# Adding a half head's three parts on TensorE and keeping the attention output in columns

## What is computed

```python
x = x + 0.5 * ffn(layernorm(x))     # shared experts of width 704, top 2 of 8 routed experts of width 352
x = x + attention(layernorm(x))
x = x + 0.5 * ffn(layernorm(x))

# attention: sequences of s tokens, 16 query heads and 4 key heads of 32
q = (x @ Wq.T).reshape(b, s, 16, 32);  k, v = (x @ Wk.T), (x @ Wv.T)   # 4 heads each
q, k = rope(q), rope(k)
attn = softmax(q @ k.T * 32 ** -0.5)
out = (attn @ v) @ Wo.T
```

## Time and profile before

| | |
|---|---|
| median of three runs | 1663.07 us (1660.93 to 1664.69) |
| the profiled execution | 1678.58 us, span of the core 1676.7 us |
| TensorE matmul | busy 1602.0 us (96%) |
| TensorE weight load | busy 1171.4 us (70%) |
| VectorE | busy 889.7 us (53%) |
| ScalarE | busy 649.7 us (39%) |
| GpSimd | busy 920.0 us (55%) |
| mean granted TensorE clock | 0.983 |

### The profile page before, as it was taken

One profiled execution on the slowest core, in us unless ns is written; L12 is line 12 of the kernel. 1 busy time (PEld: TensorE's weight loads), 2 busy tenths in 40 slices (PEclk: granted clock), 3 DMA queues, 4 the chain that ended last, 5 costly groups with the idle time before them and its releaser, 6 DMA issues.

```text
span 1676.7 us, 24265 instructions
## 1 busy us (share of the span) xinstructions
PE 1602.0 (96%) x8548; PEld 1171.4 (70%) x8548; DVE 889.7 (53%) x1534; ACT 649.7 (39%) x974; POOL 920.0 (55%) x754
## 2 busy tenths in 40 slices
PE   6998999999998898999999999989999999999997
PEld 5776799999986774444444444337778788999985
DVE  5553322222267687888888887656554432222236
ACT  4421222323232415656666566653541222323320
POOL 3106294503766856777778778750314366533635
PEclk9999899999999999999999999999999999999998
DMA  9306454423363331010010110004103455333337
GB/s 339 123 12 231 152 187 137 175 76 129 123 210 111 82 74 41 21 38 20 23 37 20 26 33 1 20 7 154 56 1 121 144 226 179 133 130 129 135 95 238
DMA packets 67841, 175.69 MB, mean 105 GB/s; under 512 B 10769, under 2 KB 11665, under 8 KB 65425
## 3 DMA queue, kind: packets, MB, share of 16 engines
q1 hardware_dynamic: 54896, 100.48, 18.5%
q0 software_dynamic: 12832, 73.67, 12.4%
HBM read 102.29 MB, written 55.84 MB: 94 GB/s over the span
## 4 chain that ended last, share of the span: by engine, by line
PE 78%; DMA 8%; DVE 5%; ACT 3%; issue 3%; POOL 2%; SPq 1%; DVEq 0%; POOLq 0%; ACTq 0%
PE PS L1117 10%; PE PS L1119 10%; PE PS L1118 10%; PE PS L1350 8%; PE PS L1331 8%; PE PS L1364 6%; PE PS L1373 5%; DMA xn<-x_routed 4%; DMA xs<-x_routed 2%; PE PS L1254 2%; PE PS L1259 2%; PE PS L1257 2%; PE PS L1256 2%; PE PS L1255 2%; PE PS L1258 2%
## 5 line engine op out<-in xcount | busy, mean ns | idle before, releaser
L1610 ACT ACTIVATE PT<-PS 128x1024 f32<-128x1024 f32 x256 | 258.0, 1022 | 157.6 <-PE PS L1350 155.4
L1907 DVE TENSOR_REDUCE nmf_later<-PS 128x1 f32<-128x1024 f32 x160 | 192.1, 1217 | 47.7 <-PE PS L1331 47.7
L1364 PE MATMUL PS<-PT,V 128*32 128x512 f32 x1024 | 203.4, 607 | 0.0
L943 POOL TENSOR_TENSOR added<-PT 128x1024 f32<-128x1024 f32 x60 | 146.3, 2439 | 102.7 <-ACT PT L1610 102.7
L1968 POOL TENSOR_TENSOR W<-raw,W 128x544 fp32r<-128x544 f32 x144 | 190.1, 1352 | 1.5
L1350 PE MATMUL PS<-QS,KS 98*128 98x512 f32 x512 | 181.7, 438 | 1.6 <-DVE nmf_later L1907 1.3
L1331 PE MATMUL PS<-KS,QS 96*128 96x512 f32 x512 | 168.7, 411 | 4.7 <-ACT PT L1610 2.3
L1874 DVE TENSOR_TENSOR thid<-thid,PS 128x352 f32<-128x352 f32 x78 | 40.6, 521 | 247.3 <-ACT thid L1541 247.3
L1350 PEld LDWEIGHTS PS<-QS,KS 98*128 98x128 f32 x512 | 80.5, 191 | 106.2 <-issue 50.0
L1956 POOL DMA_DIRECT2D raw<-ffn_w x18 | 10.0, 555 | 257.6 <-POOLq L1954 193.6
L1117 PE MATMUL PS<-xh,W 128*128 128x512 f32 x352 | 141.4, 402 | 5.6 <-ACT hid L1532 2.1
(11 more groups left out here) (197 smaller groups left out, 3874.1 us busy)
## 6 DMA issues: line engine op xcount, KB each, us to landing
raw<-ffn_w POOLq DMA_DIRECT2D x18, 2176.0 KB, 10.3
y_routed<-ytile SPq DMA_DIRECT2D x78, 256.0 KB, 2.1
xn<-x_routed SPq DMA_DIRECT2D x40, 256.0 KB, 3.4
x_routed<-xq SPq DMA_DIRECT2D x1, 9984.0 KB, 29.3
xs<-x_routed SPq DMA_DIRECT2D x38, 256.0 KB, 3.6
QS<-later_hi SPq DMA_DIRECT2D x112, 64.0 KB, 2.0
raw<-ffn_w SPq DMA_DIRECT2D x6, 768.0 KB, 10.0
raw<-ffn_w SPq DMA_DIRECT2D x16, 272.0 KB
```

Source lines behind the costliest of these rows:

```text
L943: e.tensor_tensor(to, PT[:, (u + 1) % PTBUF, :], PT[:, (u + 2) % PTBUF, :], ALU.add).then_inc(done.sem, 1)
L1364: e.matmul(PS[i * QUARTER:(i + 1) * QUARTER, ob, :], V[:, b * QT + kt, g, :], PT[:, u % PTBUF, kt % 2 * GRP:(kt % 2 + 1) * GRP], start=rou ...
L1610: e.activation(PT[:, u % PTBUF, :], PS[:, i:i + 2, :].rearrange("p b n -> p (b n)"), ACT.Exp, scale=SCALE).then_inc(p_ready.sem, 1)
L1907: e.tensor_reduce(row_maxima(n)[:, h, t:t + 1], PS[:, i:i + 2, :].rearrange("p b n -> p (b n)"), AX.X, ALU.max, negate=True).then_inc(max_ ...
```

## The change

Nothing is transposed any more between the values and the projection. The sums' matmul takes 32 columns of ones and writes the sum to all 32 rows of quarter 3. `store_head` is one matmul of OT's first 96 rows against `thirds`, three identities of 32 one below the other, into quarter 2 of the bank MISC; it stands ahead of the last value round of the half head after. VectorE takes the reciprocal of OT's quarter 3, 32x512, in an item of its own (`invert`, after the fourth unit), and multiplies PSUM by it straight into qtok, which now holds columns (32 partitions of a head, 512 tokens). ScalarE copies 128 rows to OT and waits for the reciprocal of the half before. `turn_heads` becomes `split_heads`: ScalarE and VectorE split from SBUF, without TensorE. `place_max` moves from a half head's fourth unit to the next one's first, `turn_queries` and `place_queries` two units later.

```diff
-        if outputs and pair == 0:
-            work.append(("store_head", *outputs.pop(0)))
-        if hh >= 0 and pair in (1, 2):
-            work.append(("values", hh, pair))
+        if hh >= 0 and pair == 1:
+            work.append(("values", hh, 1))
+        if hh >= 0 and pair == 2:
+            if hh:
+                work.append(("store_head", hh - 1))
+            work.append(("values", hh, 2))
+        if hh >= 0 and pair == 3:
+            work.append(("invert", hh))
...
-            e.matmul(PS[SUMS_ROW:SUMS_ROW + 1, ob, :], one_col[:], src,
+            e.matmul(PS[SUMS:, ob, :], ones[:], src,
...
-            for j in range(TPG):
-                mm = e.transpose(PS[:, MISC, j * P:j * P + SUMS_ROW + 1], OT[0:SUMS_ROW + 1, j * P:(j + 1) * P],
-                                 identf[0:SUMS_ROW + 1, 0:SUMS_ROW + 1])
+            e.matmul(PS[SUMMED, MISC, :], thirds[:], OT[0:SUMS, :],
+                     start=True, stop=True).then_inc(parts_summed.sem, 1)
...
-            e.activation(OT[0:SUMS_ROW + 1, :], PS[0:SUMS_ROW + 1, out_bank(n, hf), :],
+                act.wait_ge(parts_summed, hh - 1)
+                act.wait_ge(inverted, hh - 1)
+            e.activation(OT[:], PS[:, out_bank(n, hf), :], ACT.Copy).then_inc(ot_ready.sem, 1)
...
-            dve.step(e.reciprocal(rL[:, q, :], o[:, :, 0, 3]))
-            e.tensor_reduce(head[:, q, :, :], o[:, :, :, 0:3], AX.X, ALU.add).then_inc(halves_summed.sem, 1)
+            dve.wait_ge(parts_summed, hh)
+            dve.wait_ge(inverted, hh)
+            e.tensor_tensor(qtok[h * HD:(h + 1) * HD, t0:t0 + TPG, g * P:(g + 1) * P],
+                            PS[SUMMED, MISC, :].rearrange("p (j n) -> p j n", n=P),
+                            rL[SUMMED, :].rearrange("p (j n) -> p j n", n=P), ALU.mult)
...
+            elif kind == "invert":
+                dve.wait_ge(ot_ready, hh)
+                    dve.wait_ge(head_ready, hh - 1)
+                e.reciprocal(rL[SUMMED, :], OT[SUMS:, :]).then_inc(inverted.sem, 1)
...
-                to_columns(3, t, qtok[:, t, :], 4 + t % 4)
+                e.activation(XH[g][:, :, cols], qtok[:, t, :].rearrange("p (c n) -> p c n", c=DC),
+                             ACT.Copy).then_inc(x_hi.sem, 1)
```

More of the change, by code:

```diff
@@ L48 @@
 QUARTER = P // 4
-SUMS_ROW = 3 * QUARTER
+SUMS = 3 * QUARTER
+SUMMED = slice(2 * QUARTER, 3 * QUARTER)
 QKV = D + 2 * NKV * HD
@@ L421, in order_of_work @@
     work.append(("heads_start",))
-    outputs, maxima, lows = [], [], []
+    maxima, lows = [], []
     groups = len(KV_GROUPS)
@@ L457, in order_of_work @@
     hh = end // (QT // 2) - 1
-    work.extend([("sum", hh), ("values", hh, 0), ("store_head", *outputs.pop(0)), ("values", hh, 1), ("values", hh, 2),
-                 ("store_head", *half_head(hh))])
+    work.extend([("sum", hh), ("values", hh, 0), ("values", hh, 1), ("store_head", hh - 1), ("values", hh, 2),
+                 ("invert", hh), ("store_head", hh)])
     work.append(("attention_end",))
@@ L470, in order_of_work @@
         if i < NT:
-            work.append(("turn_heads", turned[i]))
+            work.append(("split_heads", turned[i]))
         if i >= 2:
@@ L586, in macaron @@
     nmf_first, behind = place("nmf_first", (P, REP, QT), F32, behind)
-    one_col, _ = place("one_col", (P, 1), F32, behind)
+    ones, behind = place("ones", (P, QUARTER), F32, behind)
+    thirds, _ = place("thirds", (SUMS, QUARTER), F32, behind)
     ropeS, _ = place("ropeS", (P, QT, 2, HD), F32, at)
@@ L612, in macaron @@
     MT, at = place("MT", (QT, 2, 2, P), F32, at)
-    rL, at = place("rL", (P, 2, TPG), F32, at)
-    head, at = place("head", (P, 2, TPG, HD), F32, at)
+    rL, at = place("rL", (P, GRP), F32, at)
     nmf_later, at = place("nmf_later", (P, 2 * REP, QT), F32, at)
@@ L865, in macaron @@
                 x_back[g].plan()
[L866 to L867 removed]
+        elif kind == "split_heads":
+            for a in (x_hi, x_lo):
                 a.plan(3, *key)
@@ L962, in macaron @@
     place_place = {key: i for i, key in enumerate(placed)}
[L963 to L966, removed]
     def slots_over(lane):
@@ L974, in heads_over @@
         lane.wait_ge(pv_done, last_half, 2)
-        lane.wait_ge(ot_turned, *heads[-1])
-        lane.wait_ge(ot_ready, *ends[-1])
-        lane.wait_ge(head_ready, *heads[-1])
+        lane.wait_ge(head_ready, last_half)
         lane.wait_ge(wo_ready, DC - 1)
@@ L2024, in gpsimd_program @@
             elif kind == "value_ones":
-                e.memset(one_col[:], 1.0).then_inc(v_ones.sem, 1)
+                for i in range(3):
+                    of = slice(i * QUARTER, (i + 1) * QUARTER)
+                    pool.step(e.tensor_copy(thirds[of, :], identf[of, of]))
+                    pool.after_step()
+                e.memset(ones[:], 1.0).then_inc(v_ones.sem, 1)
                 pool.wait_ge(v_ones)
```

76 lines of the change are left out of this document (35 added, 41 removed).

## The result

The changed kernel takes **1817.83 us** (median of 4 runs, 1811.97 to 1822.26) beside 1662.97 for the kernel before on the same chip: a ratio of 1.093, 95% interval [1.089, 1.097]. It is slower by 9%. The prediction was 1815 us. The profiled execution took 1814.38 us, its span is 1812.6.

A forecast was written before the change was run, and what follows sets the result against it. The prediction took TensorE to bound the kernel before, and VectorE with its long reciprocal after. Its terms, 139 + 16 - 3 = +152 us, added to the median of 1663.07, gave 1815 us, range 1740 to 1870.

The forecast's parts named there:

- the bound moves to VectorE: Attention, per half head: VectorE needs 8.8 us of work against 7.4 for TensorE, so VectorE becomes the bound.
- the loop: Attention: scores of unit 2 wait for maximum 0 behind the reciprocal; period 9.24 us, TensorE idle about 1.67 per half head.
- The reciprocal: VectorE, 32x512 per half head: 6.75 ns per element over 146 ns, 3.6 us, from a line through two small sizes.
- the rival that takes the small rows for a fixed start: VectorE: 512 elements take about 0.7 us, TensorE stays the bound; 1640 us, chance 0.08.
- the one with 8.4 ns: VectorE: reciprocal slower per element, 4.4 us for 512, 0.8 more per half head; 1863 us, chance 0.12.
- The clock: TensorE after stalls: 1.34 us lost per drop, in two half heads of three, 0.89 per half head; period 10.13.
- The rival's price: Attention: TensorE's clock stays up in spite of the stalls; 1760 us, chance 0.17.
- the term of 139: First seven groups: period from 7.65 to 10.13 us over 56 half heads, drops of the clock included; +139 us.
- The last group: Sums' matmul waits for VectorE's additions behind the reciprocal, 2.8 us, four times: 11, with clock drops 16 us.
- The end: Last OT copy and output projection: +1.7 us for the longer path, -4.7 for the transposes gone; -3 us.
- The matmul with `thirds`: TensorE: 0.01 us beside its neighbours; the rival has it run alone, 0.98 us, 1870 us in all, chance 0.07.
- The faster case: Attention: a cheap reciprocal, below about 2 us, leaves TensorE the bound; 1640 us, chance 0.08.

The follow-up runs named there:

- busy2: Changed kernel with the maximum matmuls of each half head's second unit issued three times in place of once; 1768.53 us, ratio 1.065 to the kernel before.
- r384: Changed kernel, reciprocal covering only 384 of 512 columns from the second half head on (2.55 us); 1721.96 us, ratio 1.036 to the kernel before.
- r4: Changed kernel, reciprocal covering only 4 of 512 columns from the second half head on (0.17 us); 1644.54 us, ratio 0.989 to the kernel before.
- split4: Changed kernel with the reciprocal cut into four of 128 columns, one behind each of the half head's four maxima; 1853.59 us, ratio 1.108 to the kernel before.
- defer_dve: Changed kernel, but division deferred one group: a 128x128 reciprocal per half head, multiplication on VectorE; 1709.97 us, ratio 1.023 to the kernel before.

## Why the prediction was right

**What bounds the kernel.** That TensorE was full before and had nothing to hide a wait behind held. The changed kernel shows VectorE between 88 and 91% busy ("above 90%" was expected) and TensorE idle until a maximum. VectorE's work was put at 8.8 us per half head; busy between the first and the 56th copy it is 9.0. With the clock up (busy2) that is 9.0 of a period of 9.34. So "the bound moves to VectorE" says nearly all of it. The prediction went by its other account, the loop; the two lay 0.44 us per half head apart, 25 us of its sum, and no run tells by which of them the period is set.

**The reciprocal.** Forecast 6.75 ns per element and 146 ns, 3.6 us. Measured 6.25 ns and 147 ns, 3.35 us. The line through two small sizes held over a factor of 32 in length, and the rival that takes the small rows for a fixed start (1640 us) fell, as did the one with 8.4 ns. The Trainium skill (VectorE: DVE Perf Modes, walkthrough of the 8-slice pipeline) names a repeat count of 8 for this operation. Read as eight cycles an element at its 0.96 GHz that would be an estimate of 4.3 us. The runs show 6.25 ns, six such cycles; the measurement decides.

**The loop.** Forecast 9.24 us; with the clock up, busy2 has 9.34 in the mean. From VectorE's start on maximum 3 to the scores of unit 2 it is 5.91 us (931.93 to 937.84), where I had 5.85: the reciprocal was 0.25 too long in the forecast, but I had let the maximum, the reciprocal and the next maximum overlap by 0.12 each, and they do not (1.26 and 3.38 from start to start, in place of 1.11 and 3.48). From those scores to the next maximum 3 it is 2.71 in r384 (934.84 to 937.55), forecast 2.72. The stall is longer than 1.67 because VectorE took up maximum 3 a full 1.00 us after TensorE had started it (930.93 to 931.93), behind the product, and not after 0.67, and because TensorE's own work in the loop was put 0.15 too long. In this half head the loop is thus 6.91 + 2.71 = 9.62 long, and not 9.24; 9.27 is the usual distance of two copies in busy2, where maximum 3 is taken up after 0.66.

**The clock.** Forecast 0.89 us per half head, from one case with a stall of 1.32 us. Measured 10.19 - 9.34 = 0.85 in the mean. The mechanism was named rightly, but the price rested on one case and the share on a guess. In the profile of the changed kernel 33 of the 55 distances of two copies are over 9.9 us, which none is in busy2: a share of 0.60 for the 0.67, and 47 / 33 = 1.42 us each for the 1.34. That both came out near is luck: 13 stalls of 1.38 to 1.47 us in r384, longer than the one case, lowered nothing. The rival's price was good too: 1760 for a clock that stays up, 1768.53 in busy2. Its condition did not hold.

**The period before** was taken from one half head, 7.65, and "56 half heads are like that" was wrong. The mean of 55 is 7.81 (429.3 / 55). 11 of them take 8.14 to 8.17 with TensorE busy throughout, since the transposes of queries for a later group (L1311) and of maxima (L1340) stand among their matmuls; one of 9.34 has the stall of the earlier trace rows. So the term of 139 was in truth 131.3: the new period was 0.06 above the forecast, the old one 0.16, and the distances are 55 and not 56.

**The last group.** Forecast +16, measured +19.8. The wait is where it was said to be: the sums' matmul stands still until VectorE's additions are done, in each half of odd number. GpSimd, VectorE and TensorE in the timeline of the changed kernel answer to the earlier trace rows:

```profile
1208.07 1.22 DVE L953 TENSOR_TENSOR added<-added,PT 128x1024 f32<-128x1024 f32 x1
1208.34 3.14 POOL L950 TENSOR_TENSOR added<-PT 128x1024 f32<-128x1024 f32 x1 [2.30 <-ACT PT L1606]
1209.32 2.71 DVE L955 TENSOR_TENSOR added<-added 128x512 f32<-128x512 f32 x1
...
1212.09 1.90 PE L1374 MATMUL PS<-added,ones 128*32 128x512 f32 x2 [3.90 <-DVE added L955]
...
1264.17 0.69 DVE L955 TENSOR_TENSOR added<-added 128x512 f32<-128x512 f32 x1
```

The term that was too small is the short addition. I took 0.69 us from the earlier trace rows. Shifted by the reciprocal it now begins beside an addition of GpSimd, and takes 2.71 (the same at 1227.77 with 2.78 and at 1246.30 with 2.71); it ends 0.55 us after that addition each time. The last, with GpSimd idle, takes 0.69.

**The end.** Forecast -3, measured -2.7, but not by the terms of the sum. From the last copy of OT to the first matmul with Wo it is 6.4 us (1266.9 to 1273.3), as forecast, though with a reciprocal 0.25 shorter. From the first matmul with Wo to the last it is 51.25 us, and 54.92 before: the transposes gave back 3.7 and not 4.7. The 0.7 that is left lies behind the projection, where the change does nothing. So the 1.7 - 4.7 of the forecast is in truth 1.7 - 3.7 = -2.0, and the nearness of -2.7 is luck.

**The rivals.** The matmul with `thirds` does run beside its neighbours, 96 rows deep or not. TensorE's timeline at full clock, the second half of a round:

```profile
929.39 0.62 PE L1374 MATMUL PS<-added,ones 128*32 128x512 f32 x1
929.82 0.59 PE L1381 MATMUL PS<-OT,thirds 96*32 96x512 f32 x1
929.83 0.60 PE L1365 MATMUL PS<-PT,V 128*32 128x512 f32 x2
929.84 0.59 PE L1374 MATMUL PS<-added,ones 128*32 128x512 f32 x1
930.36 0.73 PE L1351 MATMUL PS<-QS,KS 98*128 98x512 f32 x2
```

From the first half's sums to the next scores it is 0.97 us, as the earlier trace rows had it without that matmul. The faster case was said to decide at a reciprocal of about 2 us. That was too high: the periods of r4 and r384 give 1.5, and 256 elements, at 1.75 us, already stand at no change (1.002). It was worked out from VectorE's work, and that was put too low: in r4, with 0.17 us for the reciprocal, VectorE is already busy for 5.9 us per half head.

## What to carry over

A reciprocal is paid by its elements per partition, here 6.25 ns each: turn a row of sums to where there are few per partition, or pack several rows' sums over the partitions, before dividing. Add up the whole queue of the engine that gets the long operation, since here 9.0 us of work set a period of 9.34, and check who waits for what stands behind it. When an operation is deferred off such a loop, look at three things: who waits behind it on its engine, who wants the buffer that it reads, and, for VectorE's operations with two operands in SBUF, what GpSimd is doing when they begin.

## What the runs showed of the hardware

- **More work, less time.** Two repeated matmul pairs per half head made the kernel 49 us faster (1768.5 against 1817.8), because TensorE's clock stayed at 2.4 GHz. The length of a stall alone doesn't say whether the clock falls. Between the first and the 56th copy the changed kernel has 39 stalls of 1.88 to 2.23 us: behind 28 of them it fell to 1.2 GHz (as at 937.84), behind 11 it did not. r384 has 30 stalls of 1.08 to 1.10 us and 13 of 1.38 to 1.47, and it fell behind none of these. Yet 1.32 us was enough, there at 1101.4 and in the kernel before.
- **A reciprocal does not overlap its neighbours.** Two maxima back to back overlap by 0.12 us, a maximum and a reciprocal by nothing. Its time is the same for 32 and for 128 partitions: 128 elements take 0.95 us on 32 (split4) and 0.94 on 128 (defer_dve).
- **Two operands in SBUF beside GpSimd: whoever is first goes on.** All 52 products of 128x128 of defer_dve that began during an addition of GpSimd ended 0.147 to 0.154 us behind it, and the four that began with GpSimd idle took 0.29 us. In the kernel before, where the product (L1841) has two such operands too, it took from 0.29 to 1.85. The addition of 128x512 took 2.7 against 0.69 and ended 0.55 behind GpSimd's. The other way round, VectorE's addition of 128x1024 at 1208.07, begun 0.27 us before GpSimd's, kept its 1.22; GpSimd's then took 3.14. In the two other halves like it GpSimd's took 3.15 and 3.22, and 2.39 to 2.46 in all the rest. Copies from PSUM beside the same additions kept their 0.69 (L1858).
